# Cross-attention and quantised FFN on one core: a reordered opening

## The chip, the core and the metric

The kernel runs on one core of a Trainium2 chip. The metric is the device time of the whole kernel in microseconds (us), the median of the runs. The core has TensorE (PE) for matmuls and transposes, VectorE (DVE), ScalarE (ACT) and GpSimd (POOL), each with an instruction queue of its own that works strictly in order, and a queue on SyncE (SP) that issues most transfers. The engines meet only at semaphores.

## The reference

```python
def reference(x, ctx, pos, mask, Wq, Wk, Wv, Wo, kernel, bias):   # x, ctx: (32, 64, 512)
    h = layernorm(x)
    q = (h @ Wq)    # 32 heads of 128
    k, v = ctx @ Wk, ctx @ Wv      # 8 heads of 128, each for 4 heads of q
    q = q * cos[pos] + rotate_half(q) * sin[pos]     # k likewise
    attn = softmax(where(mask == 0, -1e9, q @ k.T / sqrt(128)))
    x = x + (attn @ v) @ Wo
    return x + layernorm(x) @ dequantise(quantise_mxfp4(kernel)) + bias
```

All tensors are float32.

## The kernel before, in words

**Precision.** A float32 product is made of three fast ones. Each operand is split into a high half (ScalarE casts it to the fast type) and a low half (VectorE or GpSimd subtracts the high half from the original), and TensorE sums high x high, high x low and low x high in one PSUM bank (helper `three`, L510 to L512). QR, KR, UR, OR and CR are the loaded weights and context; QH and QL, and so on, are their halves; XH and XL are the halves of the normalised and transposed x.

**Work and order.** The 2048 rows of x are 16 tiles x(0) to x(15) of 128 rows. A loop over `n` staggers the stages: `project_q(n)` makes the q projection of head `n % 4` of step `n // 4` (512 rows by one head, 12 matmuls), later stages of the same `n` make scores, softmax, values and the output projection of earlier ones. Every engine has its own copy of this loop, written out by hand, so the order on each queue is the order of the Python text. Four PSUM banks of `proj` go round among q, k, v projections and transposed x tiles; a use waits until the bank's last reader has signalled (`bank`, `freed`).

**Opening, for x(0) to x(3).** VectorE first clamps the positions (`idx`, L1076 to L1080), which need the load `pos`, then takes mean and variance of a tile (`statistics`, three small instructions). GpSimd raises the variance to the power -1/2 (`inverse`, L1235). VectorE writes the normalised tile into `qT` (`normalise`, L936). TensorE transposes it (`turn_x`, L524), with dummy transposes between (`keep_warm`, L686). ScalarE casts it to XH (`x_high`, L762) and VectorE subtracts to XL (`x_low`, L953). `project_q(0)` needs XL of all four tiles and the low half QL of its weights, which GpSimd makes (`low`, L1245).

**Rope tables.** GpSimd issues one indirect transfer for each x tile (`gather`, L1254) that collects the tile's cosine and sine rows by position; before, it issues each of the first three ahead of a power, and the fourth after VectorE's fourth normalise. TensorE turns them (`turn_rope`, L548) and ScalarE copies them to COS and SIN (`rope`, L786 and L787). `turn_rope(0)` to `turn_rope(3)` stand right behind `project_q(0)` on TensorE, then `turn_x(4)`, `project_q(1)`, `turn_rope(4)`, `turn_x(5)`, `project_q(2)`, `turn_rope(5)`, `turn_x(6)`, `project_q(3)`, `turn_rope(6)`, `turn_x(7)`, `project_k(0)`, `project_q(4)`.

**x(4) to x(7)** are already normalised by ScalarE (`x_normalise`, L767: one ACTIVATE with scale 1/sigma and bias -mean/sigma). VectorE makes that bias (`shift_mean`, L948) after GpSimd's power for two tiles at once (`inverse_pair`, L1240). GpSimd's queue between the fourth gather and the power for x(4) and x(5) is: `low` of QL 0, `gather(4)`, `low` of QL 1, `inverse_pair(4)`; behind it `low` of QL 2, `inverse_pair(6)`, `gather(5)`, `low` of QL 3.

**Elsewhere in the opening.** The q projections 0, 1 and 3 are rotated with two half-height products by sine on VectorE (`times_sin`, L1001) behind `times_cos` (L1016); the others by way of ScalarE (`exchange`). Some context tiles have their high halves copied to PSUM (`to_psum`, L754), from where VectorE makes the low halves (L960).

Of the kernel before, what the change touches and what calls it, by code (L numbers as in the profile page):

```python
# [11 lines left out]
I32 = mybir.dt.int32  # L12
# [107 lines left out]
def streamed(n):  # L120
    return [i for i, w in enumerate(STREAM) if w[0] == n]
# [45 lines left out]
def tiles(s):  # L167
    return [8 * (s // 16) + 4 * (s % 2) + t for t in range(4)]


def build(nc, x, ctxT, pos, mask, wq, wk, wv, wo, fkT, fbias, table, eye, out):
    ctx = ExitStack()
    with ctx:
# [42 lines left out]

        shift_last = tiny[:, 10:11]

        shift = tiny[:, 16:20]
        nmx, rsum, rinv = tiny[:, 12:16], tiny[:, 16:20], tiny[:, 20:24]  # L220
        idx = tiny[:, 28:44]
        amax, pw = tiny[:, 44:60], tiny[:, 60:76]
# [51 lines left out]
        def lo_made(i):  # L274

            return (v_lo if lo_on_dve(i) else g_lo), lo_count(i)
# [54 lines left out]
            return t3 if s else bias  # L331

        def x_shift(T):
            return shift_last if T == 15 else shift[:, T - 4:T - 3]

        def on_act(T):

            return {4: 1, 5: 2, 6: 3, 7: 4, 15: 5}.get(T)

        def x_source(T):  # L340
            return acc[:, T, :] if T < 8 else rawx[:, T % 2, :]
# [164 lines left out]
        def _(pe):  # L506
# [20 lines left out]
            def turn_x(T):  # L527
                b = bank(("x", T))
                if on_act(T):
                    pe.wait_ge(a_xn, on_act(T))  # L530
                else:
                    pe.wait_ge(v_xn, T + 1 if T < 4 else T - 3)
                turn(b, x_norm(T), 4).then_inc(e_xt, 1)

            def turn_f(f):
# [37 lines left out]
            def project_q(n):  # L573
                s, h = n // 4, n % 4
                b = bank(("q", n))
                c = slice(512 * (s % 2), 512 * (s % 2) + 512)
                pe.wait_ge(*lo_made(PLACE["q", s // 2, h]))
                if h == 0 and s % 16 < 2:
                    pe.wait_ge(v_xl, tiles(s)[3] + 1)
                three(proj[:, b, :], [(QH[:, h, k], QL[:, h, k]) for k in range(4)],  # L580
                      [(XH[:, k, c], XL[:, k, c]) for k in range(4)]).then_inc(e_qp, 1)

# [155 lines left out]
        def _(act):  # L738
# [6 lines left out]
            def to_psum(s, t):  # L745

                i = PLACE["c", s, t]

                if s and t < 3:
                    act.wait_ge(*lo_made(PLACE["c", 0, t + 1]))  # L750
                else:
                    act.wait_ge(a_cs, 16 if s else 2 * t)
                act.wait_ge(a_hi, i + 1)
                act.copy(psum_high(s, t), weight("c", s, t)[0].bitcast(F32)).then_inc(a_cp, 1)  # L754

# [23 lines left out]
            def rope(T):  # L779
# [6 lines left out]
                act.copy(COS[:, c], cs_turned(T)[:, 0, :]).then_inc(a_cs, 1)  # L786
                act.copy(SIN[:, c], cs_turned(T)[:, 1, :]).then_inc(a_cs, 1)  # L787

            def v_high(n):
                s, t = v_tile(n)  # L790
                v = v_count(s, t)
                b = BANK["v", v - 1]
                act.wait_ge(e_vp, v)
                if s >= 2:
                    act.wait_ge(e_pv, 4 * (s - 2) + t + 1)
                for i in range(2):
                    act.copy(VS[ROWS[i], i, 4 * (s % 2) + t, :], proj[ROWS[i], b, 0:256]).then_inc(a_vh, 1)

            act.dma_start(acc[:, 0, :], x[0]).then_inc(d_x[0], 16)
            x_high(0)  # L800
            high([0])
            x_high(1)
            high([1])
            x_high(2)
            x_high(3)

            def out_high(m):
                act.wait_ge(e_pv, m + 1)
# [14 lines left out]
            for n in range(FIRST, END):  # L823
                m = n - 5

                if n - 1 in X_AT and X_AT[n - 1] < 8:
                    x_high(X_AT[n - 1])
                if n in (1, 2):
                    to_psum(0, n)
                if 0 <= n - 1 < PAIRS and n - 1 not in ALONE:  # L830
                    exchange(n - 1)
                if n == 5:
                    to_psum(1, 3)
                if v_tile(n - 1):
# [11 lines left out]
                if n:  # L846
                    high(streamed(n))
                    if n == 4:
                        to_psum(1, 0)
                        to_psum(1, 1)  # L850
                else:
                    high(streamed(0)[:4])
                    x_normalise(4)
                    for T in range(4):
                        rope(T)
                    high(streamed(0)[4:])
                    x_normalise(5)
                if n in X_AT and X_AT[n] == 15:
                    x_normalise(15)
# [29 lines left out]
                    out_high(m - 2)  # L889
                if n in ROPE_AT:  # L890
                    rope(ROPE_AT[n])
                if n == 2:
                    to_psum(0, 3)
                if n == 4:
                    to_psum(1, 2)

# [2 lines left out]
        def _(dve):  # L899
# [171 lines left out]

            for i in range(2):
                dve.memset(PL[ROWS[1 - i], i, :].bitcast(F32), 0.0).then_inc(v_const, 1)

            dve.wait_ge(d_pos, 16)
            dve.tensor_scalar(pw, idx.bitcast(I32), 0.0, 512.0, ALU.is_lt, ALU.mult).then_inc(v_idx, 1)  # L1076
            dve.wait_ge(v_idx, 1)
            dve.tensor_tensor(amax, idx.bitcast(I32), pw, ALU.add).then_inc(v_idx, 1)
            dve.wait_ge(v_idx, 2)
            dve.tensor_scalar(idx.bitcast(U32), amax, 0.0, 511.0, ALU.max, ALU.min).then_inc(v_idx, 1)  # L1080
            statistics("x", 0)
            statistics("x", 1)
            normalise("x", 0)
            statistics("x", 2)
            normalise("x", 1)
            statistics("x", 3)
            normalise("x", 2)
            normalise("x", 3)
            for T in range(4):
                x_low(T)  # L1090
            for T in range(4, 7):
                statistics("x", T)
            shift_mean(4)
            shift_mean(5)
            statistics("x", 7)
            for n in range(FIRST, END):
# [16 lines left out]
                if v_tile(n - 1):  # L1113
# [5 lines left out]
                        made = dve.tensor_tensor(VS[ROWS[1 - i], i, 4 * (s % 2) + t, :], proj[ROWS[i], b, 0:256],  # L1119
                                                 VS[ROWS[i], i, 4 * (s % 2) + t, :].bitcast(F32), ALU.subtract)  # L1120
                    made.then_inc(v_vl, 1)
                if n - 1 in X_AT:
                    x_low(X_AT[n - 1])
                if n - 1 in FFN_AT:
                    f_low(FFN_AT[n - 1])
# [1 line left out]
                    normalise("f", FFN_AT[n])  # L1127
                if n == 0:
                    low(PLACE["c", 0, 0])
                    for T in range(6, 8):  # L1130
                        shift_mean(T)
                if n in X_AT and X_AT[n] == 11:
                    normalise("x", 11)
                if n in X_AT and X_AT[n] == 15:
# [8 lines left out]
                if 0 <= n < PAIRS:  # L1143
                    s, h = n // 4, n % 4
                    dve.wait_ge(e_qp, n + 1)
                    if s >= 2:
                        dve.wait_ge(e_qk, 4 * (s - 2) + 4)
                    if h == 0 and s % 16 < 2:
                        dve.wait_ge(a_cs, 2 * tiles(s)[3] + 2)
                    if s == 0:  # L1150
                        dve.wait_ge(e_xt, 4)
                    if s == 1:
                        dve.wait_ge(e_xt, 6)
                        dve.wait_ge(e_ct, 8)
                    times_cos(BANK["q", n], qT[:, s % 2, :, h, :], s % 2).then_inc(v_qc, 1)
                    if n in ALONE and n < 4:
                        if n > 1:
                            dve.wait_ge(g_qr, n - 1)
                        else:
                            dve.wait_ge(e_ct, 4)  # L1160
                        times_sin(BANK["q", n], qx_place(n), 0).then_inc(v_qs, 1)
                if n == 1:
                    low(PLACE["c", 0, 1])
                if n == 2:
# [63 lines left out]
        def _(pool):  # L1228
# [57 lines left out]
                pool.wait_ge(v_ks, s + 1)  # L1286
                pool.tensor_tensor(kT[:, s % 2, :], kT[:, s % 2, :], kx_place(s)[:, :], ALU.subtract).then_inc(g_kr, 1)  # L1287

            for T in range(3):
                gather(T)  # L1290
                inverse("x", T)
            inverse("x", 3)

            pool.wait_ge(v_xn, 4)
            gather(3)
            low(PLACE["q", 0, 0])
            gather(4)
            low(PLACE["q", 0, 1])
            inverse_pair(4)
            low(PLACE["q", 0, 2])  # L1300
            inverse_pair(6)
            gather(5)
            low(PLACE["q", 0, 3])
            for n in range(FIRST, END):
                if is_last(n):
                    inverse("f", FFN_AT[n])
                    add_bias(FFN_AT[n])
                if n in X_AT and X_AT[n] >= 8:
                    inverse("x", X_AT[n])
                if n in FFN_AT and not is_last(n):  # L1310
                    inverse("f", FFN_AT[n])

                lows = [i for i in (streamed(n) if n else ()) if not lo_on_dve(i)]
                while n % 8 == 0 and lows and STREAM[lows[0]][1] == "o":
                    low(lows.pop(0))
                if 0 <= n - 1 < PAIRS - 1:
                    rotate_q(n - 1)
                if n == 1:
                    gather(6)
                    low(PLACE["k", 0, 0])  # L1320
                if n == 2:
                    gather(7)

                if n == 4:
                    rotate_k(0)
                for i in lows:
                    low(i)
                if n == PAIRS - 1:
                    rotate_q(n)
                if n in FFN_AT and not is_last(n):  # L1330
                    add_bias(FFN_AT[n])
                if n == HALF - 7:
                    gather(8)
                    gather(9)
                if n in ROPE_AT and 8 <= ROPE_AT[n] < 14:
                    gather(ROPE_AT[n] + 2)
                if k_step(n):
                    rotate_k(k_step(n))
# [37 lines left out]
```

## Time and profile before

| | us |
|---|---|
| median of 3 runs | 1144.91 (1144.56 to 1145.09) |
| the profiled execution | 1145.23 |
| its span, first to last instruction | 1143.1 |
| TensorE busy | 1130.4, 99% of the span |
| start of the first projection matmul | 13.45 |

The execution's time is 2.1 us more than its span; that part lies outside the trace. Every position below is in microseconds from the start of the span. In the timeline a row is one run of like instructions: start, duration, engine, line, operation, tiles, shapes, count, and in brackets the idle time before it and what ended it. Matmuls overlap, so the distance between two starts is what one costs, not its duration.

### The profile page before, as it was taken

To read this page: it belongs to the slowest core of one execution; us is meant where nothing else is said; L and a number is where in the kernel's file an instruction comes from. 1 tells how busy PE (TensorE), PEld (TensorE's weight loads), DVE (VectorE), ACT (ScalarE), POOL (GpSimd) and SP (SyncE) were. 2 spreads that over 40 slices of the span, in tenths; PEclk is the share of its full clock that TensorE was granted. 3 is DMA by queue.
4 is the path that set the end of the run, shared out by engine and by line. 5 is a ranking of instruction groups with operands and counts; after the bars stand their busy time and mean duration, and the time that the engine had idled before them with its cause. 6 is when DMAs were issued, how large, how long until landed. Compare 5 with 4: busy or idle time off the path is not lost.

```text
span 1143.1 us, 19747 instructions
## 1 busy us (share of the span) xinstructions
PE 1130.4 (99%) x6346; PEld 973.7 (85%) x6358; DVE 812.3 (71%) x1753; ACT 766.1 (67%) x2301; POOL 629.3 (55%) x518
## 2 busy tenths in 40 slices
PE   7999999999999999999999999999999999999998
PEld 5888888888888888888888788888888888888876
DVE  8777777777777777688787766656666665666698
ACT  6866777566676766688766566676666677665663
POOL 7854655365554655579656555544655446544433
PEclk9999999999999999999999999999999999999999
DMA  8211211112111111224212221110201112020001
GB/s 260 84 30 46 74 34 51 33 43 65 37 48 33 60 38 38 93 74 138 57 53 71 84 66 56 36 49 19 84 2 36 47 38 65 12 73 20 1 4 71
DMA packets 51748, 63.47 MB, mean 56 GB/s; under 512 B 8768, under 2 KB 27584, under 8 KB 51648
## 3 DMA queue, kind: packets, MB, share of 16 engines
q1 hardware_dynamic: 50736, 59.86, 17.2%
q0 software_dynamic: 768, 2.10, 0.6%
q8 instruction: 53, 0.87, 0.3%
q14 instruction: 47, 0.39, 0.1%
q10 hardware_dynamic: 144, 0.26, 0.1%
HBM read 58.01 MB, written 4.19 MB: 54 GB/s over the span
## 4 chain that ended last, share of the span: by engine, by line
PE 93%; POOL 2%; DVE 2%; issue 1%; ACT 1%; DMA 1%; POOLq 0%; ACTq 0%; DVEq 0%
PE proj L510 15%; PE proj L511 15%; PE proj L512 15%; PE pS L613 9%; PE pO L667 9%; PE pO L668 8%; PE pO L669 8%; PE pV L645 3%; PE pV L646 3%; PE pT L628 2%; PE pO L677 2%; PE proj L564 1%; PE proj L558 1%; PE pO L680 1%; PE proj L524 1%
## 5 line engine op out<-in xcount | busy, mean ns | idle before, releaser
L870 ACT CAST PS<-pT 64x256 fp32r<-64x256 f32 x256 | 94.1, 368 | 293.4 <-PE pV L646 290.1
L1277 POOL TENSOR_TENSOR t<-t,SIN 128x512 f32<-128x512 f32 x124 | 159.8, 1288 | 189.1 <-ACT t L821 188.8
L510 PE MATMUL proj<-XH,QH 128*128 128x512 f32 x512 | 201.2, 393 | 1.2 <-POOL QL L1245 1.1
L512 PE MATMUL proj<-XH,QL 128*128 128x512 f32 x512 | 199.5, 390 | 0.0
L511 PE MATMUL proj<-XL,QH 128*128 128x512 f32 x512 | 199.3, 389 | 0.0
L667 PE MATMUL pO<-OH,AH 128*128 128x512 f32 x432 | 171.4, 397 | 0.0
L668 PE MATMUL pO<-OL,AH 128*128 128x512 f32 x432 | 169.1, 391 | 0.0
L669 PE MATMUL pO<-OH,AL 128*128 128x512 f32 x432 | 168.4, 390 | 0.0
L1281 POOL TENSOR_TENSOR qT<-qT,t 128x512 f32<-128x512 f32 x124 | 159.6, 1287 | 9.7
L1016 DVE TENSOR_TENSOR qT<-proj,COS 128x512 f32<-128x512 f32 x128 | 88.4, 690 | 94.1 <-PE proj L512 55.7
L879 ACT ACTIVATE pS<-pS,tiny 128x64 f32<-128x64 f32 x512 | 143.4, 280 | 8.9 <-DVE tiny L1179 4.6
L613 PEld LDWEIGHTS pS<-kT,qT 128*128 128x128 f32 x1024 | 133.6, 191 | 11.7 <-issue 1.9
L1287 POOL TENSOR_TENSOR kT<-kT,t 128x512 f32<-128x512 f32 x31 | 40.1, 1293 | 170.6 <-DVE t L1001 170.6
L1009 DVE TENSOR_TENSOR AL<-pV,AH 128x512 fp32r<-128x512 f32 x128 | 88.4, 691 | 61.7 <-ACT AH L811 61.4
L613 PE MATMUL pS<-kT,qT 128*128 128x64 f32 x1024 | 128.0, 268 | 1.0 <-DVE sm L1213 1.0
L1195 DVE TENSOR_TENSOR PL<-pT,PS 64x256 fp32r<-64x256 f32 x256 | 107.6, 420 | 26.4 <-ACT PS L870 22.4
L510 PEld LDWEIGHTS proj<-XH,QH 128*128 128x128 f32 x512 | 96.2, 188 | 20.9 <-DVE XL L953 1.3
L512 PEld LDWEIGHTS proj<-XH,QL 128*128 128x128 f32 x512 | 96.1, 188 | 20.3
L1245 POOL TENSOR_TENSOR OL<-OR,OH 128x512 fp32r<-128x512 f32 x62 | 79.7, 1295 | 60.9 <-ACT OH L743 60.9
L511 PEld LDWEIGHTS proj<-XL,QH 128*128 128x128 f32 x512 | 96.2, 188 | 19.3
L887 ACT CAST PS<-PS 64x256 fp32r<-64x256 f32 x256 | 103.6, 405 | 6.3
L879 ACT ACTIVATION_READ_ACCUMULATOR pS<-pS,tiny 128x1 f32 x512 | 102.1, 199 | 1.5
(197 smaller groups left out, 2562.0 us busy)
## 6 DMA issues: line engine op xcount, KB each, us to landing
QR<-wq SPq DMA_DIRECT2D x64, 256.0 KB, 2.7
OR<-wo SPq DMA_DIRECT2D x62, 256.0 KB, 3.0
CR<-ctxT SPq DMA_DIRECT2D x16, 256.0 KB, 5.1
KR<-wk SPq DMA_DIRECT2D x16, 256.0 KB
UR<-wv SPq DMA_DIRECT2D x16, 256.0 KB
acc<-x SPq DMA_DIRECT2D x15, 256.0 KB, 3.3
out<-acc SPq DMA_DIRECT2D x15, 256.0 KB, 2.0
rawx<-x SPq DMA_DIRECT2D x8, 256.0 KB, 3.0
```

Source lines behind the costliest of these rows:

```text
L510: pe.matmul(dst, lh, rh, start=k == 0, stop=False)
L511: pe.matmul(dst, lh, rl, start=False, stop=False)
L512: made = pe.matmul(dst, ll, rh, start=False, stop=k == last)
L613: made = pe.matmul(pS[:, 128 * hp + 64 * b:128 * hp + 64 * b + 64], qT[:, s % 2, 2 * p + b, 2 * hp:2 * hp + 2, :].rearrange("p h t -> p (h ...
L667: pe.matmul(pO[:, :], AH[:, m % 2, h], oh, start=h == 0, stop=False)
L668: pe.matmul(pO[:, :], AH[:, m % 2, h], ol, start=False, stop=False)
L669: made = pe.matmul(pO[:, :], AL[:, m % 2, h], oh, start=False, stop=h == 3)
L879: made = act.activation(v4[:, a], v4[:, a], ACT.Exp, bias=nmx[:, a:a + 1], accum_out=rsum[:, a:a + 1])
L887: act.copy(PS[ROWS[1 - i], i, :], PS[ROWS[i], i, :].bitcast(F32)).then_inc(a_px, 1)
L1195: dve.tensor_tensor(PL[ROWS[i], i, :], pT[ROWS[i], 0:256], PS[ROWS[i], i, :].bitcast(F32), ALU.subtract).then_inc(v_pl, 1)
L1277: pool.tensor_tensor(t[:, :], t[:, :], SIN[:, 512 * (s % 2):512 * (s % 2) + 512], ALU.mult).then_inc(g_qs, 1)
L1281: pool.tensor_tensor(dst, dst, t[:, :].rearrange("p (a t) -> p a t", t=64), ALU.add).then_inc(g_qr, 1)
```

## The change

The four first x tiles are normalised by ScalarE (`x_normalise`) as the next four already are, with VectorE's `shift_mean` in place of its `normalise`. GpSimd issues no gather before the first power, doesn't wait for VectorE's normalises before `gather(3)`, and issues `gather(5)` one `low` and one power earlier. `statistics` of x(0) goes ahead of the clamping of positions. `project_q(0)` runs its eight matmuls with QH first and waits for QL only before its last four. ScalarE's copies of the first rope tables go cosines first, then sines, and its casts, VectorE's shifts and lows, and GpSimd's two lows of UR around n = 3 and 4 are reordered.

```diff
-        shift = tiny[:, 16:20]
+        shift = tiny[:, 12:20]
...
         def on_act(T):
-            return {4: 1, 5: 2, 6: 3, 7: 4, 15: 5}.get(T)
+            return T + 1 if T < 8 else 9 if T == 15 else None
...
             def project_q(n):
-                pe.wait_ge(*lo_made(PLACE["q", s // 2, h]))
                 if h == 0 and s % 16 < 2:
                     pe.wait_ge(v_xl, tiles(s)[3] + 1)
+                if not n:
+                    for k in range(4):
+                        pe.matmul(proj[:, b, :], QH[:, h, k], XH[:, k, c], start=k == 0, stop=False)
+                        pe.matmul(proj[:, b, :], QH[:, h, k], XL[:, k, c], start=False, stop=False)
+                    pe.wait_ge(*lo_made(PLACE["q", 0, 0]))
+                    for k in range(4):
+                        made = pe.matmul(proj[:, b, :], QL[:, h, k], XH[:, k, c], start=False, stop=k == 3)
+                    made.then_inc(e_qp, 1)
+                    return
+                pe.wait_ge(*lo_made(PLACE["q", s // 2, h]))
...
+            def first_ropes():
+                for table, k in ((COS, 0), (SIN, 1)):
+                    for T in range(4):
+                        act.wait_ge(e_ct, T + 1)
+                        act.copy(table[:, 128 * T:128 * T + 128], cs_turned(T)[:, k, :]).then_inc(a_cs, 1)
...
+            x_normalise(0)
+            x_normalise(1)
             x_high(0)
+            x_normalise(2)
+            x_high(1)
+            x_normalise(3)
+            x_high(2)
             high([0])
-            x_high(1)
+            x_high(3)
             high([1])
-            x_high(2)
-            x_high(3)
...
-                if n - 1 in X_AT and X_AT[n - 1] < 8:
+                if n - 1 in X_AT and X_AT[n - 1] < 7:
                     x_high(X_AT[n - 1])
-                if n in (1, 2):
-                    to_psum(0, n)
+                if n == 1:
+                    high(streamed(0)[3:5])
+                    to_psum(0, 1)
+                    high(streamed(0)[5:])
+                if n == 2:
+                    to_psum(0, 2)
+                    to_psum(0, 3)
                 if 0 <= n - 1 < PAIRS and n - 1 not in ALONE:
                     exchange(n - 1)
+                if n == 3:
+                    x_high(7)
...
-                    high(streamed(0)[:4])
+                    high(streamed(0)[:3])
                     x_normalise(4)
-                    for T in range(4):
-                        rope(T)
-                    high(streamed(0)[4:])
+                    first_ropes()
                     x_normalise(5)
...
+            statistics("x", 0)
             dve.wait_ge(d_pos, 16)
...
-            statistics("x", 0)
             statistics("x", 1)
-            normalise("x", 0)
+            shift_mean(0)
             statistics("x", 2)
-            normalise("x", 1)
+            shift_mean(1)
             statistics("x", 3)
-            normalise("x", 2)
-            normalise("x", 3)
-            for T in range(4):
-                x_low(T)
-            for T in range(4, 7):
-                statistics("x", T)
+            shift_mean(2)
+            x_low(0)
+            shift_mean(3)
+            x_low(1)
+            statistics("x", 4)
+            x_low(2)
+            x_low(3)
+            statistics("x", 5)
+            statistics("x", 6)
...
-                if n - 1 in X_AT:
+                if n - 1 in X_AT and n not in (3, 4):
                     x_low(X_AT[n - 1])
...
                     times_cos(BANK["q", n], qT[:, s % 2, :, h, :], s % 2).then_inc(v_qc, 1)
+                    if n == 3:
+                        x_low(6)
+                        x_low(7)
...
-            for T in range(3):
-                gather(T)
-                inverse("x", T)
+            inverse("x", 0)
+            gather(0)
+            inverse("x", 1)
+            inverse("x", 2)
+            gather(1)
             inverse("x", 3)
-
-            pool.wait_ge(v_xn, 4)
+            gather(2)
             gather(3)
             low(PLACE["q", 0, 0])
             gather(4)
             low(PLACE["q", 0, 1])
             inverse_pair(4)
+            gather(5)
             low(PLACE["q", 0, 2])
             inverse_pair(6)
-            gather(5)
             low(PLACE["q", 0, 3])
...
                 if n == 4:
+                    low(PLACE["v", 0, 0])
                     rotate_k(0)
-                for i in lows:
+                    low(PLACE["v", 1, 0])
+                for i in lows if n != 3 else ():
                     low(i)
```

## Rows read from the trace of the kernel before

**Rows 1.** The page: busy time by engine, and granted TensorE clock in 40 slices

```profile
PE 1130.4 (99%) x6346; PEld 973.7 (85%) x6358; DVE 812.3 (71%) x1753; ACT 766.1 (67%) x2301; POOL 629.3 (55%) x518
...
PEclk9999999999999999999999999999999999999999
```

**Rows 2.** Waits of TensorE after 80 us: total, times, longest

```profile
PE pS L613 <- DVE sm L1213: 1.0, 2, 0.6
```

**Rows 3.** Timeline of TensorE, 0 to 36 us

```profile
4.60 1.54 PE L686 MATMUL pV<-ident 128*128 128x128 f32 x6 [4.60 <-DMA ident<-eye]
...
11.31 1.04 PE L686 MATMUL pV<-ident 128*128 128x128 f32 x8
13.45 0.47 PE L510 MATMUL proj<-XH,QH 128*128 128x512 f32 x1 [1.11 <-POOL QL L1245]
...
17.40 0.44 PE L548 MATMUL pV<-ident,t 128*128 128x128 f32 x2 [0.32 <-DMA t<-table,tiny]
17.71 0.63 PE L524 MATMUL proj<-ident,qT 128*128 128x128 f32 x4
...
20.95 0.38 PE L548 MATMUL pV<-ident,qT 128*128 128x128 f32 x2
21.30 0.63 PE L524 MATMUL proj<-ident,qT 128*128 128x128 f32 x4
...
24.31 0.39 PE L512 MATMUL proj<-XH,QL 128*128 128x512 f32 x1
25.12 0.41 PE L548 MATMUL pV<-ident,qT 128*128 128x128 f32 x2 [0.43 <-DMA qT<-table,tiny]
...
31.99 0.39 PE L510 MATMUL proj<-XH,QH 128*128 128x512 f32 x1
```

**Rows 4.** Timeline of GpSimd, 0 to 36 us

```profile
6.16 1.00 POOL L1254 DMA_INDIRECT t<-table,tiny  x1 [0.17 <-issue]
7.20 0.59 POOL L1235 TENSOR_TENSOR tiny<-tiny 128x1 f32<-128x1 f32 x1
...
11.04 1.00 POOL L1254 DMA_INDIRECT t<-table,tiny  x1 [0.86 <-DVE qT L936]
12.07 1.29 POOL L1245 TENSOR_TENSOR QL<-QR,QH 128x512 fp32r<-128x512 f32 x1
```

**Rows 5.** Transfers from 0 to 30 us: KB each, median us from issue to landing

```profile
acc<-x ACTq DMA_DIRECT2D x1, 256.0 KB, 2.8
...
t<-table,tiny POOLq DMA_INDIRECT x4, 6.3
```

**Rows 6.** The chain that ended last, in order of time, to 26 us

```profile
19.18 5.81 DMA qT<-table,tiny
```

**Rows 7.** Timeline of VectorE, 0 to 36 us

```profile
3.23 0.17 DVE L1076 TENSOR_SCALAR tiny<-tiny 128x16 f32<-128x16 int32 x1 [1.61 <-DMA tiny<-pos]
...
3.74 0.69 DVE L911 BATCH_NORM_STATS2 tiny<-acc 128x6 f32<-128x512 f32 x1
...
4.75 0.68 DVE L911 BATCH_NORM_STATS2 tiny<-acc 128x6 f32<-128x512 f32 x1
...
6.02 0.60 DVE L936 TENSOR_SCALAR qT<-acc,tiny 128x512 f32<-128x512 f32 x1 [0.19 <-POOL tiny L1235]
...
10.68 2.48 DVE L953 TENSOR_TENSOR XL<-proj,XH 128x512 fp32r<-128x512 f32 x4
...
16.51 0.34 DVE L948 TENSOR_SCALAR tiny<-tiny 128x1 f32<-128x1 f32 x2 [0.33 <-POOL tiny L1240]
...
30.93 0.69 DVE L953 TENSOR_TENSOR XL<-proj,XH 128x512 fp32r<-128x512 f32 x1
```

**Rows 8.** Timeline of ScalarE, 0 to 36 us

```profile
0.72 0.41 ACTq L799 DMA_DIRECT2D acc<-x  x1
...
10.89 1.21 ACT L762 CAST XH<-proj 128x512 fp32r<-128x512 f32 x2 [0.62 <-PE proj L524]
...
16.75 0.81 ACT L767 ACTIVATE qT<-acc,tiny 128x512 f32<-128x512 f32 x1 [0.22 <-DVE tiny L948]
```

More of the change, by code:

```diff
@@ L333, in x_shift @@
         def x_shift(T):
-            return shift_last if T == 15 else shift[:, T - 4:T - 3]
+            return shift_last if T == 15 else shift[:, T:T + 1]
         def on_act(T):
-            return {4: 1, 5: 2, 6: 3, 7: 4, 15: 5}.get(T)
+            return T + 1 if T < 8 else 9 if T == 15 else None
         def x_source(T):
@@ L531, in turn_x @@
                 else:
-                    pe.wait_ge(v_xn, T + 1 if T < 4 else T - 3)
+                    pe.wait_ge(v_xn, T - 7)
                 turn(b, x_norm(T), 4).then_inc(e_xt, 1)
@@ L751, in to_psum @@
                 else:
-                    act.wait_ge(a_cs, 16 if s else 2 * t)
+                    act.wait_ge(a_cs, 16 if s else 8)
                 act.wait_ge(a_hi, i + 1)
@@ L891, in _ @@
                     rope(ROPE_AT[n])
-                if n == 2:
-                    to_psum(0, 3)
                 if n == 4:
@@ L1077, in _ @@
             dve.wait_ge(v_idx, 1)
-            dve.tensor_tensor(amax, idx.bitcast(I32), pw, ALU.add).then_inc(v_idx, 1)
+            dve.tensor_tensor(pw, idx.bitcast(I32), pw, ALU.add).then_inc(v_idx, 1)
             dve.wait_ge(v_idx, 2)
-            dve.tensor_scalar(idx.bitcast(U32), amax, 0.0, 511.0, ALU.max, ALU.min).then_inc(v_idx, 1)
-            statistics("x", 0)
+            dve.tensor_scalar(idx.bitcast(U32), pw, 0.0, 511.0, ALU.max, ALU.min).then_inc(v_idx, 1)
             statistics("x", 1)
-            normalise("x", 0)
+            shift_mean(0)
             statistics("x", 2)
-            normalise("x", 1)
+            shift_mean(1)
             statistics("x", 3)
-            normalise("x", 2)
-            normalise("x", 3)
-            for T in range(4):
-                x_low(T)
-            for T in range(4, 7):
-                statistics("x", T)
+            shift_mean(2)
[7 more added lines that the diff above has]
+            statistics("x", 6)
             shift_mean(4)
@@ L1129, in _ @@
                     low(PLACE["c", 0, 0])
-                    for T in range(6, 8):
-                        shift_mean(T)
                 if n in X_AT and X_AT[n] == 11:
@@ L1147, in _ @@
                         dve.wait_ge(e_qk, 4 * (s - 2) + 4)
-                    if h == 0 and s % 16 < 2:
+                    if n == 0:
+                        dve.wait_ge(a_cs, 4)
+                    elif h == 0 and s % 16 < 2:
                         dve.wait_ge(a_cs, 2 * tiles(s)[3] + 2)
@@ L1160, in _ @@
                             dve.wait_ge(e_ct, 4)
+                            dve.wait_ge(a_cs, 8)
                         times_sin(BANK["q", n], qx_place(n), 0).then_inc(v_qs, 1)
+                if n == 0:
+                    for T in range(6, 8):
+                        shift_mean(T)
                 if n == 1:
```

## The prediction

> **What bounds the kernel.** I read the page first. TensorE is busy for 1130.4 us, 99% of the span [rows 1], so all its idle time together is under 13 us, and an edit that changes no TensorE work can win no more than part of that. Then the waits of TensorE after 80 us: only 1.0 us is put down to anything [rows 2], and the change touches nothing there. So the case is decided in TensorE's timeline up to 36 us, and whatever moves there moves the end by the same amount. Four places are to be seen in it [rows 3]: the first projection starts at 13.45; `turn_rope(3)` waits until 17.40 for the fourth gather and `turn_x(4)` follows at 17.71; `turn_x(5)` starts at 21.30 although two transposes begun at 20.95 are its only predecessor; and `turn_rope(5)` starts at 25.12 although the matmul before began at 24.31. From there to 31.99 the profile shows no wait.
>
> The other engines' timelines tell what set these. The first projection waited for two things that ended almost together: the four XL subtractions end at 10.68 + 2.48 = 13.16 [rows 7], QL 0 at 12.07 + 1.29 = 13.36 [rows 4]. The chain of waits names the gather of the sixth rope tile, 19.18 + 5.81 = 24.99, as what ended the wait at 25.12 [rows 6].
>
> **The opening, step by step.** x(0) is issued at 0.72 [rows 8] and lands 2.8 us later [rows 5], at about 3.5; before, the position clamp begun at 3.23 kept its statistics until 3.74, and one tile's statistics cost 4.75 - 3.74 = 1.01 [rows 7]. With statistics first: x(0) 3.57 to 4.58, clamp 0.51 to 5.09, x(1) to 6.10. GpSimd's first power, 0.59, ends near 5.3 and so no longer waits for a gather; `gather(0)` needs the clamp and starts at 5.4. Each gather costs 1.00 and 0.17 issue ahead of it, each power 0.59 [rows 4].
>
> VectorE: `shift_mean(0)` at 6.1 costs 0.20 (two took 0.34 [rows 7]). ScalarE: `x_normalise(0)` 6.35 to 7.15, at 0.81 each [rows 8]. Before, VectorE's own took 0.60 from 6.02 to 6.62 [rows 7]: the first tile is 0.5 later. GpSimd goes on: power 1 to 7.2, power 2 (statistics of x(2) end at 7.3) to 8.0, `gather(1)` to 9.15, power 3 to 9.75, `gather(2)` to 10.9, `gather(3)` 11.1 to 12.1. So the fourth gather is issued at 11.1 against 11.04 before [rows 4]: the wait for the normalises that is removed cost 0.86, but three of the four earlier gathers and powers are pushed back by the same amount.
>
> ScalarE then sets the pace. It takes over four ACTIVATEs and keeps its casts at 0.5 to 0.6 each (two took 1.21 [rows 8]): normalise 1 from 7.5, `x_high(0)` 8.2, normalise 2 from 8.7, `x_high(1)` 9.4, normalise 3 from 10.0 (its shift waits for power 3) to 10.85, `x_high(2)` 10.8, QH 0 11.3 to 11.85, `x_high(3)` 11.8 to 12.4. The last `x_low` ends at 13.1. QL 0 runs from 12.1 to 13.4, but only the last four matmuls need it and they come 8 x 0.23 = 1.9 us after the start, so it is covered; with that cover gone it would cost 0.3. First projection at 13.2: 0.25 earlier than 13.45.
>
> This 0.25 is lost at once. The projection and three rope turns end near 17.0, the fourth gather's rows land at 11.1 + 6.3 = 17.4 [rows 5], as before. Then `turn_x(4)` needs `x_normalise(4)`, at the end of a GpSimd queue that starts at the fourth gather and holds the same work as before: low, gather, low, power. Gather end 12.10 against 12.04 puts its shift at 16.57 against 16.51 [rows 7] and the ACTIVATE at 16.8 against 16.75 [rows 8]: `turn_x(4)` at 17.75 to 17.8. **Term 1: +0.06**, later. Its bounds: gathers 0 to 2 sit closer to the fourth; each may land up to one gather's time (1.0) later, and the statistics of x(0) may begin 0.2 later, so +0.7; below, both the landing and the queue would have to be faster, and the profile's idle 0.32 before 17.40 [rows 3] bounds that at -0.3. I take the value nearest the old rows.
>
> **`turn_x(5)`.** Two transposes cost 0.22, so 21.30 is 0.13 behind 20.95 + 0.22. What it waited for is `x_normalise(5)`, behind two CH casts and KH, which now come later; it moves forward by three casts, over 1 us. **Term 2: -0.13.** The casts then land behind it: the power for x(6) and x(7) and `gather(5)` swap places with QL 2, which ends near 19.0 and is needed at 21.6. No stall.
>
> **`turn_rope(5)`.** The matmul before it began at 24.31 and hands over after 0.23; 25.12 is 0.58 later. `gather(5)` now starts at 16.7, not 19.18, and lands near 16.7 + 5.81 = 22.5 [rows 6]. Next late would be the wait for ScalarE's copies of rope 4 (about 23.8 in the new order) or `x_normalise(6)` (23.4), both ahead of TensorE's 24.4. **Term 3: -0.58**; between 0 and -0.58, full value because both covers hold.
>
> **Behind it.** `project_k(0)` takes the bank that `exchange(2)` frees, about 28.1 in the new order against TensorE's 28.4. `project_q(4)`, now due at 31.3, needs `x_low(7)`, which before ran 30.93 to 31.62 [rows 7]: left there it would eat half of terms 2 and 3. The change puts it ahead of `times_sin(3)`, at about 29.8: covered, and 0.3 would be lost otherwise. The price is that `times_sin(3)` and with it `rotate_q(3)` end later, near 32.5; one UR low now stands before `rotate_k(0)` (to 35.0) and one behind (to 36.3), while the scores that need the rotation come at about 37.0. Cosines before sines let `times_cos(0)` start after four copies; TensorE waits for none of it. These cost nothing while those margins of 0.3 to 2 us hold.
>
> **Sum.** 0.06 - 0.13 - 0.58 = -0.65. Against the profiled execution, 1145.23 (span 1143.1 and 2.1 outside it), that is 1144.6; that execution lies 0.3 above the median of the runs, so against the median 1144.91 it gives **1144.3**. Measurement here can tell about 0.2%, 2.3 us, from no change; the forecast lies well inside that.
>
> **A rule weighed.** Before, the gather at 6.16 lay beside VectorE's normalise (6.02 to 6.62 [rows 7]) and took 1.00, as did the one at 11.04 [rows 4] beside a subtraction from PSUM. So the rows show no loss, and the sum takes none. The Trainium skill, "SBUF — State Buffer", section "SBUF: two separate sides", says that GpSimd can't write descriptors while VectorE holds the ports they share in a two-port mode. By that rule the four normalises that leave VectorE would free up to 0.5 us of GpSimd's queue and the result would be nearer 1143.8; this trace doesn't show the loss.
>
> **Rivals.**
> - *The head comes out late* (chance 0.22). The ScalarE and GpSimd order loses another 0.4 to 1.0: the fourth gather lands near 18, or ScalarE's normalise 3 slips. For it: GpSimd's queue has only 0.1 to 0.3 idle, TensorE sits waiting at 17.40 already. Against: its work up to `turn_x(4)` is unchanged in total. Time 1144.7 to 1145.3.
> - *The head wins too* (0.15). x(4)'s chain and the gather's landing are 0.3 faster and the first projection starts at 12.8 or so; nothing can win more than the idle time, 0.32 + 0.58 + 0.13, plus a start 0.7 earlier, 1.7 in all. Time 1143.2 to 1143.9. Against: the GpSimd sum above.
> - *Slower, through TensorE's clock* (0.03). In the rows the six dummies at 4.60 are some 0.21 apart and the eight at 11.31 some 0.11 [rows 3]: the first stand at the lower of the two levels (1.2 GHz), the later at 2.4, although the page's slices all say full [rows 1]. The later first transpose leaves a wider hole behind the first dummies. If the rise came only after the second projection, its 12 matmuls would cost 0.23 more each and the first with the ropes some 1.9 in all beyond the waits: 1.9 + 2.8 - 0.65 = +4.0, 1148.9. It passes 2.3 us slower if the low level reaches the fifth matmul of `project_q(1)`. Against: the dummies stay, and TensorE works between them about as much as before. The Trainium skill, "TensorE: Matmul & The Clock Gate", section "What's actually happening", says the idle state is the throttled one and activity releases it; that agrees with the spacing of these rows.
> - *The change doesn't move the rope gather* (0.03): `gather(5)` lands late again because transfers share the same engines. Time 1144.9.
> - Outside all of these, a shift of phase in the later stages that wins or loses over 1 us: 0.07. The forecast itself has 0.50.
>
> Range: from the head winning, 1143.3, to the head late, 1145.4, leaving out under 2 in 10. Chances: faster by over 0.2%, 0.04; within, 0.91; slower, 0.05.
>
> **What would show it.** First projection near 13.2 behind VectorE's XL, with its ninth matmul right behind the eighth; `turn_rope(3)` at 17.4 waiting for the gather and `turn_x(4)` near 17.8; no wait before `turn_rope(5)`; `project_q(4)` near 31.3 instead of 31.99. I am wrong if `turn_x(4)` moves by more than 0.4 either way, if `turn_rope(5)` or `project_k(0)` waits for ScalarE, or if scores wait for GpSimd's rotation.

## The result: slower by 1.7 us

| | before | after |
|---|---|---|
| median of 20 runs, us | 1144.93 (1144.34 to 1145.54) | 1146.66 (1146.16 to 1148.62) |
| ratio, 95% interval | | 1.0018 (1.0012 to 1.0025) |
| profiled execution / span, us | 1145.23 / 1143.1 | 1146.37 / 1144.3 |

The forecast was 0.65 us faster, the range 1143.3 to 1145.4. The ratio is just inside 0.2% (the two medians alone divide to 1.0015), but its interval lies wholly above 1: the change made the kernel slower.

**Profile after, waits of TensorE:** total us, times, longest.

```profile
PE proj L510 <- DVE t L1025: 1.8, 1, 1.8
PE proj L524 <- ACT qT L777: 1.2, 1, 1.2
...
PE proj L582 <- DVE XL L977: 0.6, 1, 0.6
```

The first line is new: a projection waits 1.8 us for VectorE's sine product. The second stands where TensorE waited 1.4 us for VectorE's normalise before. The two gather waits are gone from the list; of the first, a hole of 0.14 ahead of `turn_rope(3)` is left.

**Timeline of TensorE after**, to be read beside [rows 3]:

```profile
13.67 0.47 PE L582 MATMUL proj<-XH,QH 128*128 128x512 f32 x1 [0.62 <-DVE XL L977]
...
17.56 0.44 PE L548 MATMUL pV<-ident,t 128*128 128x128 f32 x2
18.02 0.63 PE L524 MATMUL proj<-ident,qT 128*128 128x128 f32 x4
...
21.25 0.38 PE L548 MATMUL pV<-ident,qT 128*128 128x128 f32 x2
21.47 0.60 PE L524 MATMUL proj<-ident,qT 128*128 128x128 f32 x4
23.91 0.50 PE L510 MATMUL proj<-XH,QH 128*128 128x512 f32 x1 [1.84 <-DVE t L1025]
...
26.77 0.38 PE L548 MATMUL pV<-ident,qT 128*128 128x128 f32 x2
...
33.58 0.39 PE L510 MATMUL proj<-XH,QH 128*128 128x512 f32 x1
```

`turn_x(4)` is at 18.02 against 17.71, `turn_x(5)` at 21.47 against 21.30. Four such transposes took 0.35 to 0.39 elsewhere in the two profiles, from their start to that of the next matmul. So `project_q(2)` was due at about 21.85; it started at 23.91, 2.06 late. `turn_rope(5)` then followed the matmul before it with no wait, which returns 0.58. `project_q(4)` is at 33.58 against 31.99. The sum 0.31 (`turn_x(4)`) - 0.14 (`turn_x(5)`) - 0.58 + 2.06 gives 1.65, and 1.59 is measured.

**Timeline of VectorE after:**

```profile
16.81 0.33 DVE L972 TENSOR_SCALAR tiny<-tiny 128x1 f32<-128x1 f32 x2 [1.28 <-POOL tiny L1274]
...
18.07 3.76 DVE L987 TENSOR_TENSOR CL<-CR,CH 128x512 fp32r<-128x512 f32 x1
21.75 0.68 DVE L1040 TENSOR_TENSOR qT<-proj,COS 128x512 f32<-128x512 f32 x1
22.46 1.39 DVE L1025 TENSOR_TENSOR t<-proj,SIN 64x512 f32<-64x512 f32 x2
```

**Timeline of GpSimd after**, the same stretch:

```profile
16.97 1.02 POOL L1288 DMA_INDIRECT qT<-table,tiny  x1 [0.19 <-issue]
18.02 1.30 POOL L1279 TENSOR_TENSOR QL<-QR,QH 128x512 fp32r<-128x512 f32 x1
19.27 0.74 POOL L1274 TENSOR_TENSOR tiny<-tiny 128x2 f32<-128x2 f32 x1
19.99 1.28 POOL L1279 TENSOR_TENSOR QL<-QR,QH 128x512 fp32r<-128x512 f32 x1
24.00 1.29 POOL L1307 TENSOR_TENSOR qT<-qT,t 128x512 f32<-128x512 f32 x1 [2.73 <-DVE t L1025]
```

This is the cause to be tested. VectorE's low of the first context tile (`CL <- CR, CH`) takes 3.76 us. The same line of the kernel before took 0.68:

```profile
17.77 0.68 DVE L963 TENSOR_TENSOR CL<-CR,CH 128x512 fp32r<-128x512 f32 x1
```

No wait is shown ahead of it: it has started and doesn't finish. It began 0.05 after GpSimd's low of QL 2. From there GpSimd runs three instructions without a hole, to 19.99 + 1.28 = 21.27, and the low ended 0.56 after that. In the kernel before, `gather(5)` stood behind the pair power; moving it forward put QL 2 at 18.0 and joined three instructions into one run. The sines behind the low free the bank that `project_q(2)` needs.

The kernel before already showed the two engines in each other's way. There QL 2 was over when the low began at 17.77, and GpSimd's power met the low instead. The first pair power of the same profile took 0.72:

```profile
15.75 0.72 POOL L1240 TENSOR_TENSOR tiny<-tiny 128x2 f32<-128x2 f32 x1
...
17.93 1.08 POOL L1240 TENSOR_TENSOR tiny<-tiny 128x2 f32<-128x2 f32 x1 [0.22 <-DVE tiny L915]
```

### The profile page after: what moved, and what is told of

Same layout as the page of the kernel before. It is cut to its first block, busy times and chain, and to the rows that moved or that the text cites. A ratio compares the mean times of both kernels' runs of the same rounds, so it can differ in the third digit from the quotient of the medians.

```text
span 1144.3 us, 19753 instructions
## 1 busy us (share of the span) xinstructions
PE 1131.3 (99%) x6346; PEld 975.1 (85%) x6358; DVE 814.4 (71%) x1753; ACT 767.4 (67%) x2305; POOL 628.8 (55%) x518
## 4 chain that ended last, share of the span: by engine, by line
PE 97%; DVE 1%; POOL 1%; issue 1%; ACT 0%; DMA 0%; DVEq 0%; ACTq 0%
PE proj L510 15%; PE proj L511 15%; PE proj L512 15%; PE pS L623 9%; PE pO L677 9%; PE pO L678 9%; PE pO L679 9%; PE pV L655 3%; PE pV L656 3%; PE pT L638 3%; PE pO L687 2%; PE pO L690 1%; PE proj L564 1%; PE proj L524 1%; PE proj L558 1%
```

## Experiments

Theory A: GpSimd's run keeps VectorE out of something that both need, when VectorE reads two SBUF operands. Rival B: the low, or what follows it, is late because of ScalarE's new order. The kernel before ran beside each, with medians of 1144.88 to 1144.94. The kernels that were timed here are within 0.2% of it, so positions in the profile carry the verdicts, with medians of 11 runs beside them.

**e1_pool_waits**

```diff
             gather(5)
+            pool.wait_ge(v_lo, 1)
             low(PLACE["q", 0, 2])
```

> Theory A: VectorE's low of the first context tile, which took 3.76 us in the changed kernel and 0.68 before, is held off by GpSimd's low of QL 2 (begun 0.05 us ahead of it) and the two instructions that follow with no gap. With GpSimd made to wait for that low, it takes about 0.7 us from 18.1, the second projection group (project_q(2)) starts near 21.9 instead of 23.91, and the kernel comes to about 1144.6, 2 us under the changed kernel and 0.3 under the one before. Rival B: the low waits for something else (its operands, ScalarE's order), and this wait only delays QL 2: low still over 2 us, time 1146.7 or more.

Measured: 1144.03 (1143.91 to 1144.98), ratio 0.9995 (0.9986 to 1.0004), 0.6 lower than expected. VectorE's timeline, then GpSimd's, then TensorE's at `project_q(2)` and `project_q(4)`:

```profile
17.94 0.68 DVE L987 TENSOR_TENSOR CL<-CR,CH 128x512 fp32r<-128x512 f32 x1
```

```profile
18.71 1.30 POOL L1279 TENSOR_TENSOR QL<-QR,QH 128x512 fp32r<-128x512 f32 x1 [0.85 <-DVE CL L987]
```

```profile
21.70 0.47 PE L510 MATMUL proj<-XH,QH 128*128 128x512 f32 x1
...
31.35 0.39 PE L510 MATMUL proj<-XH,QH 128*128 128x512 f32 x1
```

One wait, put on the engine that wasn't late, takes 2.6 us off the median of the change. `project_q(2)` starts at 21.70 without a wait. A holds, B falls. `project_q(4)` is now 0.64 earlier than in the kernel before (31.99), which is what my three terms had promised in sum (0.65). One by one they are +0.19, -0.15 and -0.58 in this profile, so they held in the main; what was wrong was the term left out.

**e2_low_later**

```diff
-                if n == 0:
-                    low(PLACE["c", 0, 0])
...
                 if n == 0:
                     for T in range(6, 8):
                         shift_mean(T)
+                    low(PLACE["c", 0, 0])
```

> The same low placed behind the sines and shifts of n = 0. Theory A: times_cos(0) starts at once near 18.6 and frees the bank near 20.7; no wait at project_q(2); the low may still stretch, but with nothing behind it that TensorE needs soon. About 1144.5. Rival B (ScalarE's new order or the rope copies delay VectorE): the wait at project_q(2) stays over 1 us and the time over 1146.

Measured: 1145.02 (1144.39 to 1145.41), ratio 1.0001 (0.9992 to 1.0010), 0.5 more than expected. There is no wait at `project_q(2)`, but the low met the next run, QL 3 and `rotate_q(0)`, and stretched there. VectorE, then GpSimd:

```profile
20.95 2.02 DVE L987 TENSOR_TENSOR CL<-CR,CH 128x512 fp32r<-128x512 f32 x1
```

```profile
19.89 1.28 POOL L1278 TENSOR_TENSOR QL<-QR,QH 128x512 fp32r<-128x512 f32 x1
21.14 1.28 POOL L1306 TENSOR_TENSOR qT<-qT,t 128x512 f32<-128x512 f32 x1
22.59 1.28 POOL L1287 DMA_INDIRECT qT<-table,tiny  x1 [0.17 <-issue]
```

The sines of q projection 1 came later by that, and `project_q(3)` waited at 25.65 for the bank they free. The gather at 22.59 began beside the end of the low and took 1.28, against 1.02 for the one before it. It is the same mechanism at another place: where the low stands doesn't matter, what runs beside it does.

**e3_gather_back**

```diff
             inverse_pair(4)
-            gather(5)
             low(PLACE["q", 0, 2])
             inverse_pair(6)
+            gather(5)
             low(PLACE["q", 0, 3])
```

> The changed kernel with gather(5) behind the second pair power again. Theory A: a gather reads no tile of QR or QH and leaves a hole in GpSimd's run, so the low ends near 20.8 if it starts behind QL 2, or 0.7 us after its start if it comes first; the wait at project_q(2) falls from 1.8 to 1 us or less, but turn_rope(5) waits again for its gather by up to 0.5. About 1145.2 to 1145.8. Rival B: the place of a gather on GpSimd's queue doesn't touch VectorE; 1146.6 or slower.

Measured: 1144.88 (1144.07 to 1145.28), ratio 0.9999 (0.9990 to 1.0008): better than expected. QL 2 ended ahead of the low, which took 0.68; the pair power that met it took 1.08, against 0.72 to 0.74 for others. GpSimd's timeline:

```profile
16.67 1.26 POOL L1279 TENSOR_TENSOR QL<-QR,QH 128x512 fp32r<-128x512 f32 x1
18.14 1.08 POOL L1274 TENSOR_TENSOR tiny<-tiny 128x2 f32<-128x2 f32 x1 [0.21 <-DVE tiny L939]
```

So far, whichever starts first has made the other take longer. `turn_rope(5)` stood at 24.95, again behind its gather.

**e4_only_gather**, the kernel before with one line moved:

```diff
             inverse_pair(4)
+            gather(5)
             low(PLACE["q", 0, 2])
             inverse_pair(6)
-            gather(5)
             low(PLACE["q", 0, 3])
```

> The kernel before with one line moved: gather(5) ahead of QL 2. Theory A: QL 2 now starts near 17.7, just ahead of VectorE's low at 17.8, and runs into the pair power and QL 3 without a gap, so the low stretches to over 3 us and project_q(2) waits about 2 us; the kernel loses 1 us or more, 1146 to 1146.5. My blind prediction's term, and rival B: only the wait of 0.58 at turn_rope(5) goes, 1144.3 to 1144.4.

Measured: 1146.81 (1145.11 to 1148.13), ratio 1.0018 (1.0009 to 1.0027), the whole loss of the change, from the very line that my term 3 counted as a gain of 0.58. VectorE's timeline:

```profile
18.06 3.73 DVE L963 TENSOR_TENSOR CL<-CR,CH 128x512 fp32r<-128x512 f32 x1
```

One of its 11 runs took 1145.11, which would fit a run in which VectorE came first; that one was not profiled.

**e6_one_psum**, the change with the low's second operand in PSUM (its result is not the low half):

```diff
-                    low(PLACE["c", 0, 0])
+                    i = PLACE["c", 0, 0]
+                    _, lo, raw, _, _, _ = weight(*STREAM[i][1:])
+                    dve.wait_ge(a_hi, i + 1)
+                    dve.wait_ge(e_qp, 1)
+                    dve.tensor_tensor(lo, raw, proj[:, BANK["q", 0], :].rearrange("p (k t) -> p k t", k=4),
+                                      ALU.subtract).then_inc(v_lo, 1)
```

> The changed kernel with the second operand of the stretched low taken from PSUM (a finished projection) and not from SBUF: the low half of the first context tile then holds a wrong value, the work is the same. Theory A, in its narrower form (VectorE is held off only where both operands lie in SBUF): the instruction takes 0.7 us, no wait at project_q(2), about 1144.1. Rival A2 (any VectorE instruction that reads or writes SBUF there is held off by GpSimd's run): it still takes over 3 us, 1146.5.

Measured: 1144.23 (1144.07 to 1144.74), ratio 0.9995 (0.9986 to 1.0004). VectorE's timeline:

```profile
17.94 0.69 DVE L1160 TENSOR_TENSOR CL<-CR,proj 128x512 fp32r<-128x512 f32 x1
```

GpSimd's QL 2 ran from 17.88 beside it, and nothing was stretched. Of the two forms, only the one with both operands in SBUF is held off.

**e8_gap_later**, the change with e1's wait two instructions later:

```diff
             low(PLACE["q", 0, 2])
             inverse_pair(6)
+            pool.wait_ge(v_lo, 1)
             low(PLACE["q", 0, 3])
```

> The changed kernel with GpSimd waiting for VectorE's low not ahead of QL 2 but after QL 2 and the pair power, ahead of QL 3. Theory A, held until the first hole in GpSimd's run: the low begun at 18.1 ends at about 20.7 (0.7 after the power's end at 20.0) and takes 2.6 us instead of 3.76; the wait at project_q(2) falls from 1.84 to about 0.8 and the time to about 1145.5. Rival: it is held by QL 2 alone or by no instruction of GpSimd; the low's length is then 1.9, or unchanged at 3.7.

Measured: 1144.34 (1144.09 to 1144.90), ratio 0.9995 (0.9986 to 1.0004). VectorE, then GpSimd:

```profile
17.86 1.79 DVE L987 TENSOR_TENSOR CL<-CR,CH 128x512 fp32r<-128x512 f32 x1
```

```profile
17.79 1.29 POOL L1279 TENSOR_TENSOR QL<-QR,QH 128x512 fp32r<-128x512 f32 x1
19.04 1.21 POOL L1274 TENSOR_TENSOR tiny<-tiny 128x2 f32<-128x2 f32 x1
```

My form of theory A was wrong here. I expected 2.6 us, to the end of the power and 0.7 more. The low took 1.79, near the rival's 1.9: VectorE got in at the end of QL 2, and the power took 1.21 for it. The power itself had nothing to wait for.

**e10_met_wait**

```diff
             inverse_pair(6)
+            pool.wait_ge(v_stat, 24)
             low(PLACE["q", 0, 3])
```

> In e8_gap_later VectorE's low got in right after QL 2, ahead of the pair power, a step earlier than I expected. Here the wait ahead of QL 3 is one that is met already (statistics of x(7)). Theory E: it takes a GpSimd instruction that cannot go yet, two behind, for VectorE to be let in at the first boundary; a met wait changes nothing: low 3.7 us, 1146.3 to 1146.7. Rival F: any extra semaphore instruction in GpSimd's queue opens the run; low 1.8 us, 1144.3.

Measured: 1146.71 (1146.22 to 1148.73), ratio 1.0019 (1.0009 to 1.0028). VectorE's timeline:

```profile
17.95 3.75 DVE L987 TENSOR_TENSOR CL<-CR,CH 128x512 fp32r<-128x512 f32 x1
```

So a wait that is met already doesn't open the run, and one at the same place that can't go yet does. The times say the same of every run: the slowest of e8_gap_later took 1144.90, the fastest here 1146.22. Why VectorE gets in at one boundary and not at another stays open.

**e5_dummies**, the change with 16 dummy transposes in TensorE's hole:

```diff
+                if n == 2:
+                    for _ in range(16):
+                        made = pe.transpose(pT[:, 0:128], ident[:, :], ident[:, :])
+                    made.then_inc(e_dw, 1)
                 if 0 <= n < PAIRS:
                     project_q(n)
```

(`to_psum(0, 2)` waits for `e_dw`.)

> The changed kernel with 16 dummy transposes into a free PSUM bank ahead of project_q(2), to fill TensorE's hole of about 2 us. Theory C: the long executions of the changed kernel (5 of 20 at 1147.7 to 1148.6 with a mean granted clock of 0.999) are those in which TensorE's clock falls to its lower level in or after that hole; with the hole filled none of 11 goes over 1147.2 and the median is 1146.3 to 1146.5. Rival D: they come from a different order of VectorE's and GpSimd's instructions; some 3 of 11 stay over 1147.5.

Measured: 1146.25 (1145.96 to 1146.69), ratio 1.0012 (1.0003 to 1.0021): none of 11 over 1146.7, the median just below the expected range. The profiled execution of e10_met_wait was one of the long ones, 1147.82 with a mean clock of 0.999, and shows what they are. Its TensorE timeline:

```profile
23.77 0.50 PE L510 MATMUL proj<-XH,QH 128*128 128x512 f32 x1 [1.82 <-DVE t L1025]
...
24.57 0.40 PE L510 MATMUL proj<-XH,QH 128*128 128x512 f32 x1
24.80 0.49 PE L511 MATMUL proj<-XL,QH 128*128 128x512 f32 x1
25.09 0.63 PE L512 MATMUL proj<-XH,QL 128*128 128x512 f32 x1
25.52 0.63 PE L510 MATMUL proj<-XH,QH 128*128 128x512 f32 x1
```

Its windows: TensorE, weight loads, VectorE, ScalarE and GpSimd busy, granted clock, transfer share, GB/s.

```profile
20.00:24.00 4.00, 2.18 (x13) 1.68 (x12) 3.92 (x7) 2.87 (x7) 1.28 (x2) 1.00 1.19 297
24.00:28.00 4.00, 4.00 (x12) 3.01 (x12) 3.92 (x7) 3.36 (x7) 3.81 (x4) 0.62 0.32 97
```

After a wait of 1.82 us the matmuls go from 0.23 apart to 0.43 until 28: the granted clock fell from 2.4 to 1.2 GHz for some 3 us. `project_q(2)` spans 4.31 (23.77 to 28.08) against 2.86 in the profiled execution of the change: 1.45 us on top of the hole.

**e7_before_two_lines and e12_four_lines**, to size the rest of the change. e7 is e4 with e1's wait. e12 also moves two lines of VectorE's:

```diff
                 if n == 0:
                     low(PLACE["c", 0, 0])
-                    for T in range(6, 8):
-                        shift_mean(T)
...
                         times_sin(BANK["q", n], qx_place(n), 0).then_inc(v_qs, 1)
+                if n == 0:
+                    for T in range(6, 8):
+                        shift_mean(T)
```

> The kernel before with gather(5) ahead of QL 2 and GpSimd waiting for VectorE's low ahead of QL 2, nothing else of the change. If ScalarE's normalising, the split sum and the other reordering bring nothing to TensorE, as my forecast of the head says, this equals e1_pool_waits but for 0.1 (turn_x(5)) and up to 0.4 at project_q(4): 1144.1 to 1144.5. If they are worth something, it stays at 1144.7 or more.

Measured: 1145.77 (1145.55 to 1147.27), ratio 1.0010 (1.0001 to 1.0019), a miss: VectorE's low took 0.68, but then

```profile
20.55 0.34 DVE L948 TENSOR_SCALAR tiny<-tiny 128x1 f32<-128x1 f32 x2 [2.12 <-POOL tiny L1240]
```

The shifts of x(6) and x(7) wait for a power that now comes behind a gather and QL 2, and the sines wait behind them; `project_q(2)` stood at 22.96.

> e7_before_two_lines lost 0.9 although its low took 0.68: in it VectorE waits 2.12 us for the second pair power ahead of times_cos(0), because the shifts of x(6) and x(7) stand there. This kernel moves these shifts behind the sines, as the change does, and nothing else. If that wait was the loss and ScalarE's normalising brings nothing, VectorE's sines end near 20.8, project_q(2) does not wait, and the time equals e1_pool_waits within 0.4: 1144.1 to 1144.4. If the rest of the change is worth over 0.5, it stays at 1144.7 or more.

Measured: 1144.45 (1144.07 to 1144.74), ratio 0.9994 (0.9985 to 1.0003), 0.05 above the expected range and 0.42 above e1, so between my two cases. The four lines give most of what e1 gives. For the rest of the change, ScalarE's normalising with it, 0.4 is left between 1144.45 and 1144.03, which these intervals don't separate from nothing.

## Why the prediction was wrong, point by point

- **First projection.** Forecast 13.2, measured 13.67, and 13.3 to 13.7 in the experiments on the changed kernel. As forecast it was ScalarE's and VectorE's chain and no longer QL 0, but the chain started later: `x_normalise(0)` began at 6.46 and not 6.35. The end of it also waited for TensorE's transposes, which still ran at the low clock (last point of this list): `x_high(3)` began at 12.21, and in e3_gather_back, where the last transposes ended 0.35 earlier, at 12.01, with the first projection at 13.47. It cost nothing here, because `turn_x(4)` waited for GpSimd's queue. The cover for QL 0, written as 8 x 0.23 = 1.9, is 1.84 by that product and 1.92 as measured, since the first matmul took 0.31.
- **Term 1, +0.06.** Measured +0.31 at `turn_x(4)`. The fourth gather was issued at 11.38 instead of 11.1; GpSimd's queue behind it did carry the 0.3 on unchanged. Direction right, within the bounds given.
- **Term 2, -0.13.** Measured -0.14 (0.31 late at `turn_x(4)`, 0.17 at `turn_x(5)`). Right.
- **Term 3, -0.58, is the step that failed.** The move of `gather(5)` did take away the wait at `turn_rope(5)`. I priced it by what it frees and named ScalarE's rope copies and `x_normalise(6)` as what could be late next; of QL 2 I only asked whether TensorE had it in time. I didn't ask what the move does to VectorE: it closed the hole in GpSimd's queue and set QL 2, which I had end near 19.0, beside VectorE's low, which the prediction doesn't price at all. The low took 3.76 instead of 0.68, and `times_cos(0)` began at 21.75 where e1_pool_waits has it at 18.54; of the 3.2 us between them, 2.06 reached TensorE. That is the term that isn't in my sum. The price was to be seen before the change, in the power that took 1.08 beside the low. e4_only_gather shows it from this line alone, e1_pool_waits removes it alone.
- **Behind it.** `project_k(0)` and `project_q(4)` met no wait, as forecast; the difference of 1.59 at `project_q(4)` is 1.57 at the first scores (39.27 against 37.70) and 1.2 in the span. The other 0.3 comes back at 549.69, where a weight load of TensorE (PEld) waited for ScalarE in the kernel before and does so neither in the change nor in e1_pool_waits. The line of the kernel before (total us, times, longest):

```profile
PEld proj L510 <- ACT t L821: 0.3, 1, 0.3
```

The medians differ by 1.7 and not by 1.2, as the profiled execution of before lies 0.3 above its median and that of the change 0.3 below.
- **The signs of being wrong** that the prediction named did not appear: `turn_x(4)` moved by 0.31 and not by over 0.4, neither `turn_rope(5)` nor `project_k(0)` waited for ScalarE, and the scores did not wait for GpSimd. No sign looked at VectorE between 18 and 22 us, where the loss arose.
- **The rule weighed.** The Trainium skill, "SBUF — State Buffer", section "SBUF: two separate sides", names a second case beside the one I weighed: the ports that VectorE and GpSimd share are also taken by a VectorE instruction with two SBUF inputs, against a GpSimd instruction that reads SBUF, and the one that starts first keeps them for its whole instruction. The runs agree: 3.76 with two SBUF operands, 0.69 with one in PSUM, and GpSimd's power at 1.08 and 1.21 where VectorE came first. By that sentence VectorE would be held to the end of one instruction, 1.3 us; the trace shows three in a row, 3.2 us, and the measurement decides. I had used only the half of the rule that spoke for the change.
- **The rival for the slower side** was TensorE's clock, placed ahead of `project_q(0)`. The clock rose late in the profiled execution of the change, but early enough for `project_q(0)`. The transposes of x(1) are, before and after:

```profile
8.47 0.66 PE L524 MATMUL proj<-ident,qT 128*128 128x128 f32 x4 [0.26 <-issue]
```

```profile
8.66 1.06 PE L524 MATMUL proj<-ident,qT 128*128 128x128 f32 x4
```

So at 8.66 it was still at the lower level, although the profile's windows give a clock of 1.00 there too; by the eight dummies at 12.01, 0.11 apart, it had risen. That the change made it late is not shown: e4_only_gather, e7_before_two_lines and e12_four_lines have the opening of the kernel before, and the same transposes took 1.11 to 1.12 in their profiles.

The clock falls again in the long executions, behind the hole at `project_q(2)`. In the change 5 of 20 runs have a mean clock of 0.999 and take 1147.68 to 1148.62; one more took 1147.65 at 1.000. The two other kernels with a wait of over 1.8 us there have such runs too, e4_only_gather 3 of 11 and e10_met_wait 4 of 11. In all that is 12 of 42, against 0 of 88 in the eight other kernels, which wait there for 1.04 us (e7_before_two_lines, whose longest run of 1147.27 has a clock of 1.000) or not at all. e5_dummies, with the stretched low but with the hole filled, is one of those eight; at 12 in 42 its 11 runs would all be short by chance in 2 of 100 cases. So it is well supported that the hole brings the long executions; that the clock falls in them is read in detail in one profile, and why it falls in some executions and not in others stays open.

## What to carry to other kernels

When an instruction is moved, look on the other engines at what it will now run beside, and not only at who waits for it. In this kernel a VectorE instruction with both operands in SBUF had no fixed price while GpSimd ran SBUF instructions without a hole: either a wait on GpSimd kept them apart, or one operand in PSUM took the conflict away. When an instruction's duration grows several times over with no wait ahead of it, suspect contention, and look at what started just before it. A small growth in the kernel before, such as a power of 1.08 us among others of 0.72, can be the same conflict seen from its cheap side.

## What the runs showed of the hardware

- One VectorE subtraction of 128x512 from two SBUF operands took 0.68 us where GpSimd waited for it or came second, and 3.73 to 3.76 beside three GpSimd instructions without a hole (1.30, 0.74 and 1.28 us). It began 0.05 to 0.08 us after the first of them. It took 1.79 when the third couldn't go yet, 2.02 when it began 1.06 into a run of two (1.28 us each), and 0.69 with one operand in PSUM.
- The reverse is small: GpSimd's power of two columns took 1.08 and 1.21 us in place of 0.72 to 0.75, and a gather 1.28 in place of 1.02.
- A wait of 1.82 us in TensorE's work was followed in one profiled execution, about 1.1 us after it resumed, by about 3 us at 1.2 GHz (0.43 between matmuls of 512 columns instead of 0.23); in the profiled execution of the change, with a wait of 1.84, it was not. Executions of this long kind were 12 of 42 in the three kernels with such a wait, and 0 of 88 in the eight others.
